# A delta-rule layer and six local-attention layers on one core: tile ends worked inside the next tile, and v moved in ten larger transfers per half tile

## The reference

```python
x = x + delta(layernorm(x))          # gated delta rule, 6 heads, key size 128, value size 32
h = layernorm(x)
for i in range(6):                   # local layers, 16 heads of 64, window 32
    h = local_attention(shift(h)) + h
    h = feed_forward(shift(h)) + h
x = x + h

def delta(x):
    q, k, v = (silu(causal_conv4(x @ W)) for W in (Wq, Wk, Wv))
    beta, g = sigmoid(x @ Wb), -exp(A_log) * softplus(x @ Wa + dt_bias)
    q, k = l2norm(q) / sqrt(128), l2norm(k)
    # per head and token: S = S * exp(g); u = (v - k S) * beta; S += k u^T; o = q S
    return (rmsnorm(o) * norm_w * silu(x @ Wg)) @ Wo
```

## Time and profile before

| what | value |
|---|---|
| median of 3 runs | 6353.76 us (6350.86 to 6374.57) |
| the profiled execution's own time | 6357.92 us |
| its span, first to last instruction | 6356.3 us |
| busy: PE, DVE, ACT, POOL | 5364.6, 4166.2, 2769.5, 2403.9 us |
| busy share: PE, DVE, ACT, POOL | 84%, 66%, 44%, 38% |
| instructions | 170336 |

### The profile page before, as it was taken

One profiled execution on the slowest core, in us unless ns is written; L12 is line 12 of the kernel. 1 busy time (PEld: TensorE's weight loads), 2 busy tenths in 40 slices (PEclk: granted clock), 3 DMA queues, 4 the chain that ended last, 5 costly groups with the idle time before them and its releaser, 6 DMA issues. The chain is left out here.

```text
span 6356.3 us, 170336 instructions
## 1 busy us (share of the span) xinstructions
PE 5364.6 (84%) x71376; PEld 3392.0 (53%) x71376; DVE 4166.2 (66%) x6338; ACT 2769.5 (44%) x5035; POOL 2403.9 (38%) x2148
## 2 busy tenths in 40 slices
PE   6877777777868686999999999999999999999994
PEld 4756566575748483455454444445545454454442
DVE  6564646565556556777777777777777777777772
ACT  3131322323231313555555555555555555555552
POOL 2231322222223223444444444444444444444440
PEclk8877878787879697999999999999999999999997
DMA  0000000000000002222222222222222222222221
GB/s 18 5 1 4 1 4 1 4 1 4 1 4 1 4 1 67 59 58 64 72 62 61 63 71 58 58 61 72 60 59 64 71 59 58 63 70 57 57 57 33
DMA packets 255851, 252.33 MB, mean 40 GB/s; under 512 B 29680, under 2 KB 248688, under 8 KB 254704
## 3 DMA queue, kind: packets, MB, share of 16 engines
q1 hardware_dynamic: 255088, 241.29, 15.1%
HBM read 29.90 MB, written 4.19 MB: 5 GB/s over the span
## 5 line engine op out<-in xcount | busy, mean ns | idle before, releaser
L1245 POOL TENSOR_TENSOR turn<-prod 128x512 f32<-128x512 f32 x768 | 983.3, 1280 | 1952.5 <-DVE prod L1285 990.0
L988 PE MATMUL banks<-w2s,xs 128*128 128x512 f32 x2304 | 1244.9, 623 | 87.6 <-DVE xs L1317 79.4
L1285 DVE TENSOR_TENSOR prod<-banks,tabs 128x1024 f32<-128x1024 f32 x768 | 935.9, 1219 | 116.5 <-ACT sq L1132 116.0
L1132 ACT ACTIVATE sq<-banks 128x512 f32<-128x512 f32 x768 | 459.3, 598 | 968.7 <-PE banks L988 965.1
L1254 POOL TENSOR_TENSOR turn<-turn,rs 128x512 f32<-128x512 f32 x768 | 832.9, 1105 | 88.1 <-ACT rs L1149 84.1
L583 POOL TENSOR_TENSOR ao<-at,msk 128x512 f32<-128x512 f32 x288 | 391.7, 1371 | 1005.9 <-PE banks L360 526.5
L1018 PEld LDWEIGHTS banks<-msk,turn 128*128 128x128 f32 x3072 | 325.5, 141 | 573.1 <-issue 563.2
L1321 DVE TENSOR_REDUCE mx<-banks 128x8 f32<-128x512 f32 x384 | 265.6, 692 | 389.9 <-PE banks L1004 387.1
L1296 DVE TENSOR_REDUCE ss<-sq 128x8 f32<-128x512 f32 x768 | 519.2, 676 | 1.5
L1018 PE MATMUL banks<-msk,turn 128*128 128x128 f32 x3072 | 483.2, 280 | 3.9 <-ACT pt L1171 1.6
L537 ACT ACTIVATE p<-banks 128x512 f32<-128x512 f32 x288 | 172.0, 597 | 719.7 <-PE banks L360 719.7
(11 more groups left out here) (204 smaller groups left out, 9858.3 us busy)
## 6 DMA issues: line engine op xcount, KB each, us to landing
v<-v_tok SPq DMA_DIRECT2D x1152, 132.0 KB
v<-v_tok SPq DMA_DIRECT2D x384, 66.0 KB
v<-v SPq DMA_DIRECT2D x188, 132.0 KB, 2.6
w2s<-in_weights SPq DMA_DIRECT2D x10, 768.0 KB, 4.7
tabs<-in_rot SPq DMA_DIRECT2D x40, 128.0 KB, 2.6
w2s<-in_weights SPq DMA_DIRECT2D x1, 2713.5 KB, 11.0
w2s<-in_weights SPq DMA_DIRECT2D x10, 256.0 KB, 3.0
xin<-in_x SPq DMA_DIRECT2D x8, 256.0 KB, 3.8
```

The lines of the kernel that those rows point to most:

```text
L988: pe.matmul(a_bank(use), xs[:, t % 2, b * P:(b + 1) * P], w[:, at:at + 512], start=True, stop=True).then_inc(a_done, 1)
L1132: a.activation(sq[:, r % 2, :], a_bank(use), ACT.Square).then_inc(sq_done, 1)
L1245: gp.tensor_tensor(turn[:, r % ROTS, :, :].rearrange(halves, s=2), prod[:, r % 2, 0, :, :].rearrange(halves, s=2), prod[:, r % 2, 1, :, :] ...
L1285: v.tensor_tensor(prod[:, r % 2, :, :, :], a_bank(use).rearrange("p (h d) -> p h d", h=HU).unsqueeze(1) .to_broadcast([P, 2, HU, DH]), tab ...
```

## The change

In the delta layer the loop over tiles is written out, from -1 to 8: block `t` works stages 2 to 4 of tile `t`, in between stage 5 of tile `t - 1` and stage 1 of tile `t + 1`. Block -1 only makes the first `xn`, block 8 only ends tile 7, each in the order of before. Where the inserted pieces stand:

- Start of the tile: VectorE `squares_o`, ScalarE `inverse_o`.
- Conv stage: VectorE `gated_o` after the first pair of chunks, `residual` after the pair of chunk 4, `centre` after that of chunk 6. TensorE `turn_o` ahead of projection 4, `output` ahead of 6, `mean_1` ahead of 8, `variance` after the last. ScalarE `take_o` ahead of chunk 4 and `square` ahead of chunk 10 of its list.
- Then ScalarE `rstd` ahead of the exponents, and VectorE `normed` into `y` ahead of the queries and keys. The transposes of v wait for `rstd`.
- In the last pair of heads: `turn_x`, `mean_x`, `variance` on TensorE in steps 1, 2 and 4; copy, square and `rstd` on ScalarE in steps 1, 3 and 5; `centre` and `normed` into `xn` on VectorE in steps 2 and 6.

`xt` and `sg` become double, and the layer norms get buffers of their own. In the local layers `v_tok` becomes a ring of two half tiles of four batches, and each half tile's v goes by 8 transfers of all four batches, issued when the fourth is there; with the 2 of the kept window they are ten. ScalarE's copies wait for the transfers of the half tile two before.

The core of the diff (what stands in the listing above and is removed, such as the old ends of the four engines' lists, is left out here, as are blocks -1 and 8, which call the same functions in the order of before):

```diff
--- before.py
+++ after.py
-with nc.Fori(0, NT) as t:
+for t in range(-1, NT + 1):
+    attend, behind, ahead = 0 <= t < NT, t >= 1, t + 1 < NT
+    LAST_LN, NEXT_LN = 1, 1 + behind
     with nc.Block(no_gpsimd_drain=True) as block:
...
+            if ahead:
+                sp.dma_start(xin[:], x[:, (t + 1) * P:(t + 2) * P, :].rearrange("b p d -> p b d"))\
+                    .then_inc(x_loaded, 16)
+                sp.wait_ge(x_loaded, 16)
+            if behind:
+                sp.wait_ge(x1_ready, 1)
+                sp.dma_start(x1_dram[:, :, (t - 1) * P:t * P], blocks(x1[:])).then_inc(x1_stored, 16)
+                sp.wait_ge(x1_stored, 16)
...
+            def turn_x():
+                pe.wait_ge(x_loaded, 16)
+                if attend:
+                    pe.wait_ge(kt_ready, H1)
+                for b in range(NB):
+                    last = pe.transpose(p[6][:, b * P:(b + 1) * P], xin[:, b, :], ident)
+                last.then_inc(x_turned, 1)
+            def mean_x():
+                pe.wait_ge(xt_ready, 1)
+                pe.matmul(p[7], mean_m, xt[:, (t + 1) % 2, :], start=True, stop=True).then_inc(mean_ready, 1)
+            def variance(n, bank):
+                pe.wait_ge(lnsq_ready, n)
+                pe.matmul(bank, mean_m, lsq[:], start=True, stop=True).then_inc(var_ready, 1)
+            def turn_o():
+                pe.wait_ge(on_ready, 1)
+                for b in range(NB):
+                    pe.transpose(p[6][:, b * P:(b + 1) * P], o[:, b, 0:P], ident)
+                    last = pe.transpose(p[7][0:VD - P, b * P:(b + 1) * P], o[:, b, P:VD], ident)
+                last.then_inc(on_turned, 1)
+            def output():
+                pe.wait_ge(ot_ready, 2)
+                pe.matmul(p[6], wo[:, 0, :], ot[:, 0, :], start=True, stop=False)
+                pe.matmul(p[6], wo[0:VD - P, 1, :], ot[0:VD - P, 1, :], start=False, stop=True)\
+                    .then_inc(wo_ready, 1)
+            def mean_1():
+                pe.wait_ge(x1_ready, 1)
+                pe.matmul(p[7], mean_m, x1[:], start=True, stop=True).then_inc(mean_ready, 1)
...
             for n in range(NCH):
                 m = P if n < NCH - 1 else VD - P
+                if behind and n == 4:
+                    turn_o()
+                if behind and n == 6:
+                    output()
+                if behind and n == 8:
+                    mean_1()
                 if n >= 4:
                     pe.wait_ge(tap_ready, n - 3)
                 pe.matmul(p[n % 4][0:m, :], w[:, n * P:n * P + m], xn[:], start=True, stop=True)\
...
+            if behind:
+                variance(LAST_LN, p[7])
...
+            if behind:
+                pe.wait_ge(rstd_ready, LAST_LN)
...
+                    elif ahead and pair + 1 == H1 // 2:
+                        if i == 1:
+                            turn_x()
+                        elif i == 2:
+                            mean_x()
+                        elif i == 4:
+                            variance(NEXT_LN, p[6])
...
+            def square(n):
+                a.wait_ge(xc_ready, n)
+                a.activation(lsq[:], xc[:], ACT.Square).then_inc(lnsq_ready, 1)
...
             def rstd(n, bank_of_var):
...
+                link(a.activation(llg[:], bank_of_var, ACT.Ln, bias=c(C_EPS)))
+                a.activation(lrs[:], llg[:], ACT.Exp, scale=-0.5).then_inc(rstd_ready, 1)
+            def take_x():
+                a.wait_ge(x_turned, 1)
+                if behind:
+                    a.wait_ge(x1_ready, 1)
+                a.activation(xt[:, (t + 1) % 2, :], p[6], ACT.Copy).then_inc(xt_ready, 1)
+            def inverse_o():
+                a.wait_ge(om_ready, 1)
+                link(a.activation(om[:, 1, :], om[:, 0, :], ACT.Ln, scale=1.0 / DV, bias=c(C_EPS)))
+                a.activation(om[:, 2, :], om[:, 1, :], ACT.Exp, scale=-0.5).then_inc(ostd_ready, 1)
+            def take_o():
+                a.wait_ge(on_turned, 1)
+                a.activation(ot[:, 0, :], p[6], ACT.Copy).then_inc(ot_ready, 1)
+                a.activation(ot[0:VD - P, 1, :], p[7][0:VD - P, :], ACT.Copy).then_inc(ot_ready, 1)
...
             a.preload_act_table_set(LN_EXP)
...
+            if behind:
+                inverse_o()
...
             for n in range(NCH + PRE):
+                if behind and n == 4:
+                    take_o()
+                if behind and n == 10:
+                    square(LAST_LN)
                 if n < NCH:
                     take(n)
...
+                a.activation(sg[:, t % 2, 2 * i:2 * i + 2, :], src[:, :, 0:VD], ACT.Silu)\
                     .then_inc(gates_taken, 1)
...
             a.preload_act_table_set(LN_EXP)
+            if behind:
+                rstd(LAST_LN, p[7])
...
+                    if ahead and not more:
+                        if i == 1:
+                            take_x()
+                        elif i == 3:
+                            square(NEXT_LN)
+                        elif i == 5:
+                            rstd(NEXT_LN, p[6])
...
+            def centre(n, src):
                 v.wait_ge(mean_ready, n)
...
+                v.tensor_tensor(xc[:], src, p[7], ALU.subtract).then_inc(xc_ready, 1)
+            def normed(n, dst):
                 v.wait_ge(xc_ready, n)
                 v.wait_ge(rstd_ready, n)
...
+                v.tensor_tensor(dst, blocks(xc[:]), blocks(lrs[:]), ALU.mult).then_inc(xn_ready, 1)
+            flat = "p b (h d) -> p (b h) d"
+            old = sg[:, (t - 1) % 2, :, :]
+            def squares_o():
+                link(v.tensor_tensor(osq[:], o[:], o[:], ALU.mult))
+                v.tensor_reduce(om[:, 0, :], osq[:].rearrange(flat, h=H1), AX.X, ALU.add).then_inc(om_ready, 1)
+                link(v.tensor_tensor(old.rearrange(flat, h=H1), old.rearrange(flat, h=H1),
+                                     over_batches(rows[:, 2 * H1:2 * H1 + DV], NB * H1), ALU.mult))
+            def gated_o():
+                v.wait_ge(ostd_ready, 1)
+                link(v.tensor_tensor(o[:].rearrange(flat, h=H1), o[:].rearrange(flat, h=H1),
+                                     along(om[:, 2, :], DV), ALU.mult))
+                v.tensor_tensor(o[:], o[:], old, ALU.mult).then_inc(on_ready, 1)
+            def residual():
+                v.wait_ge(wo_ready, 1)
+                done(v.tensor_tensor(x1[:], p[6], xt[:, (t - 1) % 2, :], ALU.add), x1_ready, 1)
...
+            if behind:
+                squares_o()
...
+                if behind and pair == 0:
+                    gated_o()
+                if behind and pair == 4:
+                    residual()
+                if behind and pair == 6:
+                    centre(LAST_LN, x1[:])
...
             for h in range(2):
                 masked_decay(h)
+            if behind:
+                normed(LAST_LN, last_block())
...
+                    if ahead and not more:
+                        if i == 2:
+                            v.wait_ge(xt_ready, 1)
+                            centre(NEXT_LN, xt[:, (t + 1) % 2, :])
+                        elif i == LEVELS - 1:
+                            normed(NEXT_LN, blocks(xn[:]))
...
-v_tok = sb("v_tok", [P, 3, 2, HU, DV1])
+v_tok = sb("v_tok", [P, 2, NB, HU, DV1])
...
-                for i in range(2):
-                    for b in (2 * i, 2 * i + 1):
-                        n = item_use(U, 8 + b)
-                        sp.wait_ge(a_free[n % 2], n // 2 + 1)
-                    slot, to = (2 * U + i) % 3, slice(2 * i, 2 * i + 2)
-                    for x in range(2):
-                        src = v_tok[:, slot, :, x * UP:(x + 1) * UP, :].rearrange("p b h d -> p b (h d)")
-                        sp.dma_start(v2[x * 64 + WIN:(x + 1) * 64, h, to, 0, :], src[0:WIN, :, :])\
-                            .then_inc(vd[h], 16)
-                        for m in range(1, NW):
-                            sp.dma_start(v2[x * 64:(x + 1) * 64, h, to, m, :],
-                                         src[(m - 1) * WIN:(m + 1) * WIN, :, :]).then_inc(vd[h], 16)
+                for b in range(NB):
+                    n = item_use(U, 8 + b)
+                    sp.wait_ge(a_free[n % 2], n // 2 + 1)
+                for x in range(2):
+                    src = v_tok[:, h, :, x * UP:(x + 1) * UP, :].rearrange("p b h d -> p b (h d)")
+                    sp.dma_start(v2[x * 64 + WIN:(x + 1) * 64, h, :, 0, :], src[0:WIN, :, :])\
+                        .then_inc(vd[h], 16)
+                    for m in range(1, NW):
+                        sp.dma_start(v2[x * 64:(x + 1) * 64, h, :, m, :],
+                                     src[(m - 1) * WIN:(m + 1) * WIN, :, :]).then_inc(vd[h], 16)
...
                 else:
                     b = i - 8
-                    W = U - 2 if b < 2 else U - 1
-                    if W >= 0:
-                        a.wait_ge(vd[W % 2], VDMA * (W // 2 + 1))
-                    a.activation(v_tok[:, (2 * U + b // 2) % 3, b % 2, :, 0:DH],
```

(14 more changed lines are left out.)

103 lines of the change are left out of this document (35 added, 68 removed).

## The result

Interleaved with runs of the kernel before, the changed kernel takes 6264.76 us (median of 4, 6262.95 to 6274.63) against 6361.45 (median of 4, 6350.86 to 6374.57): ratio 0.985, 95% interval 0.9826 to 0.9874. It is faster by 97 us, where 159 were forecast, and 10 us above the range. The profiled execution took 6262.95 us.

The account below looks back on a forecast made before the run. Delta layer bound by a chain of dependent steps, local layers by TensorE's work and waits. Boundary savings of 161 us, less 1.3 and 0.9, gave 159 off 6357.9: 6199 profiled, 6195 against the median, stated as 6200; range 6160 to 6255.

Parts of the forecast that it names:

- Denser, but rarer bursts: I take 0, with 15 us either way.: Local layers: effect of the new v transfers on TensorE's late instructions, taken as 0, 15 us either way.
- TensorE's gaps before L1004: Local layers: 101.8 us in 95 gaps with no releaser; their growth was named as a sign of a wrong prediction.
- rival 3: Local layers: the v burst becomes a wait, making the kernel slower than before, for example 6450 or 6642 us; chance 0.03.
- Net per boundary: 35.5 - 9.0 - 1.3 - 2.2 = 23.0: Delta layer: us saved per tile boundary after losses in conv stage, after it and in third pair; times 7, 161.
- Rival 2: Delta layer: clock stays up in tile start and conv stage, later stages gain too; 6160 us, chance 0.10.
- so I take 9 us: Conv stage: loss per tile from items inserted in the engines' queues, within 6.6 to 10.2 us.
- 0.4 (full clock) to 2.5 us (half): Conv stage: VectorE's loss per tile from `output()` ahead of projection 6 and `mean_1` ahead of projection 8.
- After the conv stage: Delta layer: loss per tile from late `rstd` and `normed` into `y`, taken as 1.3 us, up to 3.5 without cover.
- The third pair: Third pair of heads: TensorE's inserted transposes, mean and variance cost 2.2 us per tile, 4.4 at half clock.
- The boundary: Between tiles: last write of `y` to ScalarE's start takes 0.94 us in written-out code, against 1.63 before.
- rival 1: Delta layer: TensorE's queue order costs more, 14 us in the conv stage, gain only 90; 6265 us, chance 0.12.
- The low chance for a loss (0.03): Whole kernel: probability given to the change measuring slower than the kernel before, against 0.94 for faster.

Follow-up runs that it names:

- e2: Kernel before the change with only the changed transfers of v (delta layer as before): 6396.08 us, ratio 1.0059 to the kernel before.
- e6: Changed kernel, the second four large v transfers held until three items of the half tile before are multiplied: 6217.95 us, ratio 0.9768 to the kernel before.
- e7: e1 with `gated_o` on VectorE ahead of the first pair of taps instead of behind it: 6171.78 us, ratio 0.9699 to the kernel before.
- e11: e1 with 24 unneeded TensorE products in step 3 of the second pair of heads: 6196.55 us, ratio 0.9733 to the kernel before.
- e8: e7 with `mean_1` behind the last projection and the late layer norm's following pieces later: 6153.21 us, ratio 0.9672 to the kernel before.
- e1: Changed kernel with v moved as before the change, so only the delta layer is changed: 6232.12 us, ratio 0.9801 to the kernel before.
- e10: e1 with 24 unneeded TensorE products in step 1 of the second pair of heads: 6236.60 us, ratio 0.9782 to the kernel before.
- e12: e1 with unneeded TensorE products in the second pair of heads, 10 in step 1 and 24 in step 3: 6196.00 us, ratio 0.9720.

## Why the prediction was wrong

The direction and the mechanism in the delta layer held; 62 us of the forecast gain did not come. In the profiled executions, 95.2 us apart, 63.8 are missing: 28.6 in the local layers, 33.5 before them (30 in the periods of the tiles, the rest at the first and the last tile) and 1.5 in the fill of `v_tok` and at the end.

1. **"Denser, but rarer bursts: I take 0, with 15 us either way."** This step failed: 28.6 us lost here, 35 by e2 against the kernel before. The gaps ahead of the scores were seen and their carrier named, but the price was set by the number of bursts. What counts is how long a burst keeps all DMA engines full. The bursts of before did not (0.55); e6's four large ones did, at 0.93, but for 4 us only. The forecast's own sum had "eight of double size at most 8.8 us", that is, all 16 engines full for 8.8 us, and held it only against the time at which the data are needed; the trace has about 10 (0.82, 1.02 and 0.65 of 4 us each). That the gaps are instructions that come late is borne out by the packets of q8, above. Why they come later behind a long burst, though the packets themselves take 1.1 to 1.2 us with and without it, no run shows. The row that I named as making the prediction wrong, TensorE's gaps before L1004, is the one that grew. No burst was late for its data, as forecast; rival 3 had looked at the wait for v, not for the code.
2. **The clock was priced only where the change works.** "Net per boundary: 35.5 - 9.0 - 1.3 - 2.2 = 23.0" has no term for the stages that are not touched: this step failed too, a term put at nothing without a reason. A tile is 281.6 us on average where 277.3 was forecast: 4.3 us, some 30 over the tiles. The terms of the sum explain none of it on balance (points 3 and 4). By the order of time, it lies between the chunks' norms and the last pair: pair 1 is 3.4 us longer on average (59.1 before, then 59.6 and 65.6 by turns), pair 0 0.6, the way there 0.2. Rival 2 held that "later stages gain too"; they lost. e7 and e11 give most of it back, and neither takes any work from the pairs. What makes the long stretch at half clock come in every second tile stays open.
3. **"so I take 9 us" for the conv stage** was 10.0 and 10.5. The chain over three engines before pair 4 cost 1.9 + 4.6 - 0.6 = 5.9, inside the 4.8 to 6.3. The part of `output()` and `mean_1` together, "0.4 (full clock) to 2.5 us (half)", measured 2.7, in one wait: `mean_1` took 2.08 us for its product, at half clock, after 5.19 us of idle TensorE. 1.3 us per tile too little. e7 and e8 show both waits to be the order of the queues.
4. **After the conv stage**, 1.3 was taken and 0.15 measured: VectorE's taps end later, so that what stands behind them has less to wait for. **The third pair**: 2.2 taken, 1.7 measured; steps with an item took 6.91 and 6.97 us, others 6.11, as forecast. **The boundary**: 1.35 us instead of 0.94, between the two ends; no code came late there. With the conv stage they cancel: +1.3 - 1.1 - 0.5 + 0.3 = 0 per tile.
5. **The fill of `v_tok`**: 3.58 us instead of 2.70, the +0.9 of the sum.

The measured 6265 is the figure of rival 1, and rival 1 was not right: it had 14 us in the conv stage, which took 10, and nothing in the local layers. A number that lands says nothing about its cause. The low chance for a loss (0.03) was not put to the test by this kernel, whose gain in the delta layer covers it; e2 shows that the change in the transfers, alone, is slower by 0.6%, and the text had no case for it of its own.

## What to carry to other kernels

When a kernel is long and written out, its instructions are traffic as well: gaps with no releaser, in the middle of runs of equal instructions, are their mark, and a burst that keeps all DMA engines full for some 10 us lengthens them even where its own data come in time. Merge transfers for SP's sake only if SP is waited for, and leave a pause between halves. When work is inserted into engines' queues, put each item behind what it waits for and ahead of what waits for nobody: two moves of this kind brought what the conv stage gives back from 10 us to 1. And after a change of order read the granted clock of stages that were not touched; a stop of 4 us was paid for again in the 7 us behind it, and an order of work in one stage decided how long another ran at half clock.

## What the runs showed of the hardware that was not expected

- TensorE's stops for "issue" ahead of the scores number 89 to 96 in 3740 us in every kernel, and their sum goes from 82.9 us (paced large transfers) to 129.7 (dense burst). Their number hardly depends on the load, their length does. Each ends 1.1 to 1.7 us after 16384 bytes of instructions have landed; some 480 such packets land in the local layers, and one in five is waited for.
- The queue of instructions moved 9.36 MB in 571 packets, 16.4 KB each. The Trainium skill, "Runtime: NRT & Kernel Launch", section on instruction fetch mechanics, has blocks of 16 KiB, with which this agrees, and calls their cost mostly hidden; here the waits for them were up to 3.5% of the stretch (129.7 of 3740 us, e2).
- The same local code took 3834 to 3857 us in six kernels that differ only ahead of it (e1, e7, e8, e10, e11, e12), one execution each. In the slowest, e10, the trace has 28 stretches at half clock in 3740 us where e1 has 18 (95.6 us in all against 58.1), and 7 us more of the gaps.
- Useless products can pay: with 5.5 us of them in a stop of 3.8, a pair of heads took 57.6 us instead of 59.6 (short tiles) and 65.6 (long ones; these e7 brought to 59.6 without any).
- The large copies within SBUF, issued together, took 5.0 us from issue to landing, by the page's row, against 4.2 for the same ones in groups of four (e6), and those of half the size beside them 3.7 against 2.4.
